# A long fused layer on one core: the last stage's tensors moved to addresses by their use on TensorE

## The reference, cut to what matters

```python
def _L0_attn_ref(u, ...):                       # a state-space convolution block
    z = rmsnorm(u, pre_norm_w) @ in_proj_w.T    # 256 -> 768
    z_pre = short_convolution(z) + short_b      # 3 taps, per channel
    x2, x1, v = jnp.split(z_pre, 3, axis=1)
    xv = x1 * v
    y = (long_convolution(xv, h) + xv * D_skip) * x2
    y = y @ out_proj_w.T + u                    # 256 -> 256
    zm = rmsnorm(y, post_norm_w)
    return y + jax.nn.gelu(zm @ l1_w.T) * (zm @ l2_w.T) @ l3_w.T    # 256 -> 672 -> 256

def _L0_ffn_ref(x, W1, b1, W2, b2, scale):      # a feed-forward block, 256 -> 1024 -> 256,
    ...                                         # with products of rows of x added to W1 and W2

x = x + _layernorm(_L0_attn_ref(_layernorm(x), ...))
x = x + _layernorm(_L0_ffn_ref(_layernorm(x), ...))
```

## Time and profile before

| | |
|---|---|
| median of 3 runs | 1076.65 us (1076.63 to 1077.24) |
| the profiled execution | 1076.75 us |
| its span (first to last instruction) | 1075.0 us |
| TensorE matmul, weight load, busy share | 98%, 94% |
| VectorE, ScalarE, GpSimd, busy share | 82%, 66%, 28% |
| granted TensorE clock | full in every slice |
| matmuls | 9012 |

### The profile page before, as it was taken

How to read it: one execution, slowest core, us unless ns; L and a number is a source line. 1 busy time by engine, 2 the same in 40 slices (tenths; PEclk the granted TensorE clock), 3 DMA queues, 4 the chain that set the end, 5 groups by cost and what they waited for, 6 DMA issues and landing times.

```text
span 1075.0 us, 24951 instructions
## 1 busy us (share of the span) xinstructions
PE 1050.8 (98%) x9012; PEld 1008.5 (94%) x9012; DVE 877.8 (82%) x2322; ACT 710.8 (66%) x1589; POOL 299.5 (28%) x575
## 2 busy tenths in 40 slices
PE   8899999999999999999999999999999999999998
PEld 7777888899989999999999999989999999999997
DVE  7999998774788888888887878897888888887776
ACT  7879887764456666666666666656666666666644
POOL 7677775470101112111111111111112111111111
PEclk9999999999999999999999999999999999999999
DMA  3337977986322222233222222432222223222000
GB/s 130 120 117 236 294 216 196 363 318 151 83 66 41 54 57 50 52 52 58 59 60 58 52 51 60 122 96 41 60 51 50 52 53 59 59 58 60 21 21 31
DMA packets 112491, 102.83 MB, mean 96 GB/s; under 512 B 7552, under 2 KB 103744, under 8 KB 112112
## 3 DMA queue, kind: packets, MB, share of 16 engines
q1 hardware_dynamic: 111136, 98.67, 36.2%
q0 software_dynamic: 736, 2.51, 0.6%
q10 hardware_dynamic: 496, 0.05, 0.0%
HBM read 75.75 MB, written 30.70 MB: 99 GB/s over the span
## 4 chain that ended last, share of the span: by engine, by line
PE 67%; DVE 6%; issue 2%; ACT 1%; POOL 0%; POOLq 0%; DVEq 0%; ACTq 0%
PE ps_ring L1551 35%; PE ps_w L1551 16%; PE ps_m L1551 9%; PE ps_o L1551 4%; PE ps_rt L1566 2%; DVE base L1373 1%; PE ps_w L1561 1%; DVE bn L1277 1%; PE ps_m L1617 1%; DVE prod L1320 0%; DVE ht_l L1289 0%; DVE pt_l L1289 0%; POOL sc L1129 0%; ACT rows L1254 0%; DVE yrow L1512 0%
## 5 line engine op out<-in xcount | busy, mean ns | idle before, releaser
L1129 POOL TENSOR_TENSOR sc<-sc,small 128x2 f32<-128x2 f32 x127 | 94.5, 744 | 676.8 <-DVE sc L1501 404.6
L1194 ACT ACTIVATE gate<-ps_ring 128x256 f32<-128x256 f32 x192 | 73.0, 381 | 129.7 <-PE ps_ring L1551 128.9
L1215 ACT ACTIVATE hid<-ps_ring,small 128x256 f32<-128x256 f32 x256 | 112.1, 483 | 24.2 <-PE ps_w L1551 13.4
L1551 PE MATMUL ps_ring<-mt_l,wl_h 128*128 128x256 f32 x640 | 125.5, 277 | 2.6 <-DVE mt_l L1289 2.6
L1551 PE MATMUL ps_ring<-mt_h,wl_h 128*128 128x256 f32 x640 | 125.5, 277 | 1.8 <-DVE prod L1320 1.3
L1551 PE MATMUL ps_ring<-mt_h,wl_l 128*128 128x256 f32 x640 | 124.9, 277 | 0.0
L1289 DVE TENSOR_TENSOR ht_l<-hid,ht_h 128x256 fp32r<-128x256 f32 x256 | 103.1, 423 | 16.5 <-ACT ht_h L1219 10.6
L1551 PE MATMUL ps_ring<-xt_h,we_h 128*128 128x256 f32 x512 | 104.8, 285 | 2.5 <-DVE prod L1320 2.4
L1551 PE MATMUL ps_ring<-xt_h,we_l 128*128 128x256 f32 x512 | 101.3, 279 | 0.0
L1551 PE MATMUL ps_ring<-xt_l,we_h 128*128 128x256 f32 x512 | 101.3, 279 | 0.0
L1320 DVE TENSOR_TENSOR prod<-ps_ring,gate 128x256 f32<-128x256 f32 x192 | 80.7, 420 | 24.2 <-ACT gate L1194 20.6
(11 more groups left out here) (203 smaller groups left out, 2720.2 us busy)
## 6 DMA issues: line engine op xcount, KB each, us to landing
toep_scratch<-taps_scratch SPq DMA_DIRECT2D x26, 512.0 KB, 7.4
toep<-toep_scratch SPq DMA_DIRECT2D x26, 512.0 KB, 8.8
xa<-in_x SPq DMA_DIRECT2D x16, 512.0 KB, 4.9
x_scratch<-x2c SPq DMA_DIRECT2D x16, 512.0 KB, 3.7
x2s<-x_scratch SPq DMA_DIRECT2D x32, 256.0 KB, 6.7
xa_c<-in_x SPq DMA_DIRECT2D x32, 256.0 KB, 2.7
xb_c<-in_x SPq DMA_DIRECT2D x32, 256.0 KB, 2.7
yin<-seq SPq DMA_DIRECT2D x124, 64.0 KB, 5.5
```

Of the source, the lines that this page charges most:

```text
L1129: nc.gpsimd.tensor_tensor(sc[:, to], sc[:, to], neg_half[:, 0, 0:CC], ALU.pow).then_inc(S[done], 1)
L1194: nc.scalar.activation(gate[rows_of, m % 2], ring[m % RING][rows_of, 0], ACT.Gelu_apprx_tanh).then_inc(S["gate_done"], 1)
L1215: nc.scalar.activation(hid[:, m % HIDS], block_of, ACT.Gelu, bias=b1s[:, m:m + 1]).then_inc(S["hid_done"], 1)
L1551: mm = nc.tensor.matmul(out, lhs(a, kk), rhs(b, kk), start=(j == 0), stop=(closed and j == len(todo) - 1))
```

## The change

Unused tensors of 64 bytes (`HALF_LINE = 16` floats) are allocated between groups of tensors, and a few allocations are reordered. No instruction is added, removed or moved.

```diff
+HALF_LINE = 16
...
+        def half_line(ctx, name):
+
+            sb(ctx, name, [P, HALF_LINE])
+
...
+        half_line(whole, "streamed0")
         ident = sb(whole, "ident", [P, P])
...
         wout = [sb(whole, f"wout_{s}", [P, KB, D], F32R) for s in "hl"]
+        wl3 = [sb(whole, f"wl3_{s}", [P, FULL, D], F32R) for s in "hl"]
+        wstack = sb(whole, "wstack", [3 * REST, D], F32R)
+
+        half_line(whole, "loaded0")
         wl1 = [sb(whole, f"wl1_{s}", [P, KB, FULL * P], F32R) for s in "hl"]
         wl2 = [sb(whole, f"wl2_{s}", [P, KB, FULL * P], F32R) for s in "hl"]
 
         wrest = [sb(whole, f"wrest_{s}", [P, KB, 2 * REST], F32R) for s in "hl"]
-        wl3 = [sb(whole, f"wl3_{s}", [P, FULL, D], F32R) for s in "hl"]
-
-        wstack = sb(whole, "wstack", [3 * REST, D], F32R)
...
-    OFFSET = 16
...
-        we1_high, we2_high = (sb(ctx, name, shape, F32R) for name, shape in
-                              (("we1_h", [P, KB, H]), ("we2_h", [P, HB, D])))
+        half_line = v["half_line"]
+        we1_high = sb(ctx, "we1_h", [P, KB, H], F32R)
+        half_line(ctx, "streamed1")
+        we2_high = sb(ctx, "we2_h", [P, HB, D], F32R)
+        half_line(ctx, "loaded1")
         with ExitStack() as weights_made:
             base1 = sb(weights_made, "base1", [P, KB, H])
+            half_line(weights_made, "streamed2")
             base2 = sb(weights_made, "base2", [P, HB, D])
         we1 = [we1_high, sb(ctx, "we1_l", [P, KB, H], F32R)]
+        half_line(ctx, "streamed3")
         we2 = [we2_high, sb(ctx, "we2_l", [P, HB, D], F32R)]
         b2s = sb(ctx, "b2s", [P, D])
-        sb(ctx, "offset", [P, OFFSET])
         xa = sb(ctx, "xa_c", [P, CC, D])
         xb = sb(ctx, "xb_c", [P, CC, D])
         x2s = v["x2s"]
-        yt = [sb(ctx, f"yt_{s}", [P, KB, TC], F32R) for s in "hl"]
         yrow = sb(ctx, "yrow", [P, 2, CC, D])
-        rows = sb(ctx, "rows", [P, CC, D])
         zt = [sb(ctx, f"mt_{s}", [P, KB, TC], F32R) for s in "hl"]
         xt = [sb(ctx, f"xt_{s}", [P, KB, TC], F32R) for s in "hl"]
         gate = sb(ctx, "gate", [P, 2, TC])
         prod = sb(ctx, "prod", [P, 2, TC])
+        half_line(ctx, "loaded2")
+        rows = sb(ctx, "rows", [P, CC, D])
+        yt = [sb(ctx, f"yt_{s}", [P, KB, TC], F32R) for s in "hl"]
         pt = [sb(ctx, f"pt_{s}", [P, FULL, TC], F32R) for s in "hl"]
```

## The result

The changed kernel takes 1084.68 us (median of 6 runs, 1083.79 to 1085.32), against 1076.98 us of the kernel before on the same chips: a ratio of 1.0065, 95% interval 1.0051 to 1.0080. It is slower by 7.7 us where 5.1 us less were forecast. The profiled execution took 1083.83 us with a span of 1082.1.

What follows compares the result with a forecast made beforehand. TensorE was taken to bound the last stage, by matmul count times spacing. Gains of 4.5 + 0.3 + 0.2 + 0.1 = 5.1 us gave 1071.6 us; 8-in-10 range 1068.0 to 1079.5.

Steps and rivals of the forecast that it cites:

- (a): ffn_up, entered by a turn in its own layout: 5.48 us instead of 5.66, times 25 = 4.5 us gained.
- (b): out_projection: the switch of layout ahead of it goes, 1.37 us to 1.36, about 0.3 us gained in all.
- (c): Down projections: 0.2 us gained after the second making of weights (5.66 against 5.46), 0.1 us on the last one.
- (d): Turns, 0.44 us each before and after: 0 taken, bound 1.5 us either way.
- (e): Starts of mlp_down and ffn_down behind the 96-row wstack matmul, in one layout already: 0, perhaps 1.1 us less.
- (f): The two weight-making stretches, run on the chain of VectorE, ScalarE and GpSimd: slow spacing there is covered, 0.
- (g): Whether another engine limits once TensorE is faster: a step of 24.35 us against VectorE's 20.3, no wait, 0.
- (h): First two stages, where seq and ident move to 64: 0, bound 0.6 us either way.
- (i): DMA reads of seq starting 64 bytes off: the 124 large ones hidden, one small gather perhaps exposed; 0, bound 0.2 us loss.
- the slow mode spreads: ffn_down's second chunk enters slow and hands the mode to mlp_block: 11 us more, 1087.5 us, chance 0.17.
- No change: ffn_up stays slow because of the turn as such or mlp_block's 64-column block: 1076.0 to 1076.7 us, chance 0.18.

Runs made afterwards that it cites:

- the kernel with everything at 192: The changed kernel with every loaded tensor of the last stage at 0 modulo 256 and every streamed one, ident included, at 192: 1081.34 us, ratio 1.0047.
- the kernel at 1071.8 us: The changed kernel with we2_h alone moved from 192 to 64 modulo 256: 1071.81 us, ratio to before 0.9953.

## Why the prediction was wrong, point by point

- The bound, that in plain steps the time is the matmuls' count times their spacing: right. 6.4 of the 7.1 us of span are spacing there.
- Two spacings, 113.3 and 117.9, a mode entered and kept: right, and seen in every run.
- (a) ffn_up at 5.48 us: measured 5.46 and 5.48, the size is right. The reason given, that the turn now has its own layout, is wrong: with ident moved in the kernel with everything at 192 no steady step changed, and in the kernel before the same turn goes with 5.47 when only xt is moved. The spacers did two other things to ffn_up: they made its difference 192 in the passes with we1_h, and put we1_h and we1_l 128 bytes apart modulo 256. Either alone freed it in the kernel before (5.47 with xt moved, 5.46 with we1_l moved). In the kernel at 1071.8 us the step is what frees it: made alike, 5.66 is back. In the changed kernel no run parts the two; the pieces of 5.48 get fast behind the step, those of 5.46 ahead of it. So that the size came out was luck.
- (b) out_projection 1.36: right. (c), the down projection behind the second making of weights: forecast 5.46, measured 5.60 on the chain, so 0.06 us gained and not 0.2; the last one stayed at 2.37. (d), the turns: 0.44 both times, right.
- **The step that failed is (e)** with the layout count behind it: "in one layout today already. 0". The layouts were compared modulo 128, where the changed kernel is uniform. Modulo 256 it is not: ffn_down's passes with we2_h went from 192 to 64. It was priced at zero and cost 0.09 + 0.07 us in ffn_down and 0.30 in mlp_block, which inherits: 0.46 a step.
- (f) was put at 0; the second making of weights took 0.7 us more, with a DMA read of 5.04 us on the chain that was not there before. Why it is there stays open.
- (g), (h), (i): no wait of TensorE in plain steps; the changed kernel stood 0.35 us ahead of the kernel before when plain steps began, inside (h)'s bound; the reads of seq took 6.0 us for 5.5, hidden, and the small ones of 8 KB 2.2 us for 1.9; no run separates what the one on the way into the last stage cost. The Trainium skill's rule (DMA: Bandwidth & Descriptors, How a descriptor splits into AXI transactions) had the sign right: 18 beats for 16, an eighth by that estimate, 9% measured.
- The rival *the slow mode spreads* named the place and the way (ffn_down's second chunk above 2.8 us, handed to mlp_block) and had 0.17. Its reason, a property of 0/64 modulo 128, was refuted by the kernel at 1071.8 us, which is 0/64 modulo 128 throughout. Its 1087.5 us (its own terms give 1087.7) missed that ffn_up would be gained at the same time, and that ffn_down's first chunk would be slow too.
- *No change* rested in part on the Trainium skill (TensorE: Matmul & The Clock Gate, Part 2), by which the weight load takes nothing from the running matmul. The runs disagree with what was drawn from it, that an address could not matter: addresses alone moved this kernel from 1071.8 to 1092.6 us.

The range's upper end, 1079.5, left the spreading case out; that case was cheaper than it was priced.

**What stays open.** Why addresses set the spacing at all. Why ffn_up, entered behind a turn, stays slow at difference 192 with all tensors alike (three kernels: 0/192 twice and 128/64) from the third or fourth step of a batch at the latest, but is fast in some steps ahead of that, while ffn_down's second chunk recovers in the same layout, and ffn_up did recover without a step in the kernel before with xt moved. The stage ahead (mlp_block's difference, its 64-column block) was not varied by itself.

## What to carry to other kernels

Read the spacing of each stage from the chain, time by count, before and after, and look at stages whose own addresses did not change: a mode is inherited. And a layout that is uniform by one modulus is not uniform by another; change one tensor at a time.

## What the runs showed of the hardware that was not expected

- At the full granted clock (1.00 in the last stage, before and after), alternating loads of 128 float32 columns and matmuls of 256 run at 113.3 or 117.8 ns with nothing between for whole stages, by the difference of starts and by what came before. Difference 0: 120 ns (fillers); 32, 128, 160, 224: 117.0 to 118.7; 64 and 192: either mode.
- Where a stage at difference 64 throughout was slow behind a disturbance (a turn, the 96-row matmul), it stayed slow to its end: 5.66 us for 48 in the kernel before, 2.83 for 24 in the changed one with we2_l moved. Not each entry is slow: ffn_up at difference 64 took 5.45 at 359.97 and 762.34 in the kernel before, behind the same turn. At 192 ffn_down recovers in all steady steps (2.73 to 2.76 us), ffn_up only in some kernels.
- With a step by 128 bytes of the loaded operand's start inside it ffn_up is fast in plain steps (5.45 to 5.53 us in six kernels, with a first difference of 64 or of 192). A step of the streamed operand did not free it (5.65, one kernel), and in another kernel the slow mode began in ffn_down at such a step (2.81).
